# Constant operands of Vector's build work in PSUM, another order of the edge batches, one table zeroed before the other, and the last layer's units inside its sweeps

## The reference, cut to what matters

```
x = LN(x + three GCN layers(x, edge_weight) @ Wl + bl)
x = LN(x + two SAGE layers(x))
x = LN(x + sigmoid(decoder(relu(5 GRU steps(encoder(x))))))
x = LN(x + one GCN layer(x, unit weights) @ W + b)
# every layer sums h[src] over the edges into dst: segment_sum(h[src] * norm, dst)
```

## Time and profile before

| | us |
|---|---|
| median of 3 runs | 5748.14 (5744.3 to 5749.56) |
| the profiled execution | 5746.37 |
| its span, first to last instruction | 5744.6 |
| PE busy | 4803.0 (84%) |
| POOL busy | 2567.7 (45%) |
| DVE busy | 1751.7 (30%) |

### The profile page before, as it was taken

The page is one execution under the profiler, slowest core; times in us unless marked ns, Lnnn a source line. Parts: engine busy times, 40 slices in busy tenths (PEclk is TensorE's granted clock), DMA queues, the critical chain, the costliest instruction groups (busy, mean ns, idle before and its releaser), DMA issues. The chain is left out here.

```text
span 5744.6 us, 79088 instructions
## 1 busy us (share of the span) xinstructions
PE 4803.0 (84%) x25665; PEld 2581.3 (45%) x25665; DVE 1751.7 (30%) x3228; ACT 1204.8 (21%) x2507; POOL 2567.7 (45%) x1704
## 2 busy tenths in 40 slices
PE   3555555496299999999999998999999999997796
PEld 3555555242145444444454544444444444443343
DVE  9999999200000100010050303103030120303413
ACT  5555556100011111111120102112020110202200
POOL 4888888888888888888885000000000000000100
PEclk7555555697699999999999999999999999999897
DMA  9999983487399999999989785775858668582474
GB/s 352 358 354 353 351 238 52 119 240 220 49 303 302 270 300 289 301 273 299 288 235 298 242 294 185 224 254 182 299 174 271 215 222 268 172 299 74 146 261 135
DMA packets 717086, 1401.96 MB, mean 244 GB/s; under 512 B 268372, under 2 KB 356264, under 8 KB 691880
## 3 DMA queue, kind: packets, MB, share of 16 engines
q1 hardware_dynamic: 483832, 1346.10, 69.9%
q0 software_dynamic: 225216, 0.70, 7.6%
q10 hardware_dynamic: 7920, 53.79, 2.4%
HBM read 1160.09 MB, written 240.25 MB: 244 GB/s over the span
## 5 line engine op out<-in xcount | busy, mean ns | idle before, releaser
L837 PE MATMUL psum<-arena 128*128 128x512 f16 (+3 forms) x14014 | 3683.0, 424 | 299.4 <-issue 171.9
L837 PEld LDWEIGHTS psum<-arena 128*128 (+2 forms) x14014 | 1671.9, 124 | 2245.1 <-issue 1113.7
L548 POOL DMA_INDIRECT W_adj<-arena x782 | 1289.3, 1649 | 257.1 <-issue 239.1
L548 POOL DMA_INDIRECT C_adj<-arena x782 | 1213.9, 1552 | 240.1 <-issue 240.0
L680 POOL TENSOR_TENSOR arena<-arena 128x512 f32 (+1 forms) x13 | 22.1, 1700 | 1811.7 <-DVE arena L1172 1811.7
L427 DVE TENSOR_SCALAR_CACHE_REDUCE arena<-arena 128x2048 bf16<-128x2048 f32 (+7 forms) x392 | 709.5, 1875 | 0.6 <-issue 0.6
L497 PE MATMUL psum<-arena 128*128 (+1 forms) x6664 | 224.6, 167 | 482.7 <-DVE arena L449 459.4
L497 PEld LDWEIGHTS psum<-arena 128*128 128x128 bf16 x6664 | 213.7, 104 | 499.2 <-issue 450.3
L1356 DVE COPY arena<-psum 128x512 f32<-128x512 f32 (+1 forms) x39 | 23.2, 653 | 1353.5 <-PE psum L847 1159.4
L270 ACT ACTIVATE arena<-arena 128x1024 bf16<-128x1024 f32 (+7 forms) x392 | 298.5, 773 | 401.3 <-DVE arena L427 387.8
L1358 DVE TENSOR_SCALAR arena<-psum,arena 128x512 f32<-128x512 f32 x30 | 21.9, 748 | 1038.9 <-PE psum L837 1038.9
(11 more groups left out here) (233 smaller groups left out, 2594.5 us busy)
## 6 DMA issues: line engine op xcount, KB each, us to landing
arena<-C_adj SPq DMA_DIRECT2D x784, 384.0 KB
arena<-W_adj SPq DMA_DIRECT2D x294, 768.0 KB
arena<-C_adj SPq DMA_DIRECT2D x392, 512.0 KB
arena<-W_adj SPq DMA_DIRECT2D x147, 1024.0 KB
arena<-C_adj SPq DMA_DIRECT2D x392, 288.0 KB
arena<-W_adj SPq DMA_DIRECT2D x147, 576.0 KB
W_adj<-arena SPq DMA_DIRECT2D x12, 6400.0 KB
W_adj<-arena SPq DMA_DIRECT2D x12, 6144.0 KB
```

Source lines behind the costliest of these rows:

```text
L548: return pool.indirect_dma_start(table, bass.IndirectOffsetOnAxis(idx[:, t:t + 1], 0), values[:, t:t + 1], None, compute_op=ALU.add)
L837: ins = pe.matmul(psum[:, bank + b, 0:width], lhs, ring[:, slot, b * BANK:b * BANK + width], start=begin and part == 0, stop=False, skip_g ...
```

## The change: what it does, and the diff

Four edits. (1) `psRamp` and `psUpto` (f32, PSUM bank 2) and `psW` (f32, banks 4 and 5) are the constant operands of the five `compare` products in place of `rampb`, `upto` and `w`. The small block that works out `flight` and `ready` becomes `conflicts()` and is called after the first `merge` instead of before the first `compare`. (2) The batches come in the order 0, then groups 4g+2, 4g+4, 4g+1, 4g+3, and 45, 47, 46, 48 at the end. Here too no neighbours touch; the inputs then need 29, 37, 45 and 49 batches for the four sweeps (counted from the inputs). (3) SP writes zeros to all of W_adj, then to all of C_adj. (4) The stage `last` goes. In sweeps 1 to 3 of `decode` PE makes, after each of the first laps of eight chunks, the product of one unit of the sweep before; DVE and ACT normalise it, and ACT issues its output DMA. The three units of sweep 3 come after it. The products read `sum_fm` directly (no ACT copy), into PSUM banks 7 and 3, and the result lies where `h_fm` was.

```diff
+ORDER = [0] + [4 * g + u for g in range((NB - 5) // 4) for u in (2, 4, 1, 3)]
+ORDER += [b for u in (0, 1) for b in range(len(ORDER) + u, NB - 1, 2)] + [NB - 1]
...
+LAST_BANKS = (7, 3)
...
+    psRamp, psUpto = psum[:, 2, 0:P], psum[:, 2, P:2 * P]
+    psW = psum[:, 4:6, :].rearrange("p a b -> p (a b)")[:, 0:TILES]
...
-        for z in range(BLOCKS):
-            at_, width = z * BANK, block_width(z)
-            for table, of, zeroed in ((W_rows, zero, w_zeroed), (C_rows, z16, c_zeroed)):
+        for table, of, zeroed in ((W_rows, zero, w_zeroed), (C_rows, z16, c_zeroed)):
+            for z in range(BLOCKS):
+                at_, width = z * BANK, block_width(z)
                 for u, (c0, c1) in enumerate(halves):
...
-        dve.tensor_copy(rampb, ramp)
-        link(dve.tensor_scalar(upto, ramp, pcol[:, 0:1], None, ALU.is_ge))
+        dve.tensor_copy(psRamp, ramp)
+        dve.tensor_copy(psW, w)
+        link(dve.tensor_scalar(psUpto, ramp, pcol[:, 0:1], None, ALU.is_ge))
...
+        def conflicts():
             (the block of L402 to L418, indented)
...
-            dve.tensor_tensor(high, rampb[:, 0:CHUNKS].unsqueeze(1).to_broadcast([P, TB, CHUNKS]),
+            dve.tensor_tensor(high, psRamp[:, 0:CHUNKS].unsqueeze(1).to_broadcast([P, TB, CHUNKS]),
...
-            dve.tensor_tensor(ohl, rampb.unsqueeze(1).to_broadcast([P, TB, P]),
+            dve.tensor_tensor(ohl, psRamp.unsqueeze(1).to_broadcast([P, TB, P]),
...
-            dve.tensor_tensor(Et[:, slot, 0:half, :], near, upto.unsqueeze(1).to_broadcast([P, half, P]), ALU.mult)
+            dve.tensor_tensor(Et[:, slot, 0:half, :], near, psUpto.unsqueeze(1).to_broadcast([P, half, P]), ALU.mult)
...
-            dve.tensor_tensor(weighted, high, w[:, b * TB:(b + 1) * TB].unsqueeze(2).to_broadcast([P, TB, CHUNKS]),
+            dve.tensor_tensor(weighted, high, psW[:, b * TB:(b + 1) * TB].unsqueeze(2).to_broadcast([P, TB, CHUNKS]),
...
-            dve.tensor_tensor(Et[:, slot, half:, :], far, upto.unsqueeze(1).to_broadcast([P, half, P]),
+            dve.tensor_tensor(Et[:, slot, half:, :], far, psUpto.unsqueeze(1).to_broadcast([P, half, P]),
...
             merge(b, b % 2)
+            if b == 0:
+                conflicts()
...
-    return stages + [("gru", STEPS - 1, None), ("decode", None, (False, "ln", True)), ("last", None, None)]
+    return stages + [("gru", STEPS - 1, None), ("decode", None, (False, "ln", True))]
...
+            def last_product(j):                       # PE
+                if j >= 2:
+                    pe.wait_ge(s["products_read"], last.read + j - 1)
+                for c in range(chunks_of(j)):
+                    ins = pe.matmul(psum[:, LAST_BANKS[j % 2], c * D:(c + 1) * D],
+                                    sum_fm[:, (j * UC + c) * P:(j * UC + c + 1) * P], wt["L3W"], start=True, stop=True)
+                ins.then_inc(s["products"], 1)
...
-                    with pe.Fori(0, LAPS) as i:
+                    lap = 0
+                    if name == "decode":
+                        for j in blocks_of(sweep - 1):
+                            for u in range(LAP):
+                                chunk(lap * LAP + (u + 1), u, sweep, 16 * lap + 16 * (laps + 1))
+                            pe.wait_ge(s["sum_dve"], base.sum_dve)
+                            pe.wait_ge(s["sum_act"], base.sum_act)
+                            last_product(j)
+                            lap += 1
+                    with pe.Fori(lap, LAPS) as i:
...
+            if name == "decode":                       # after the last sweep
+                for j in blocks_of(SPLIT):
+                    last_product(j)
...
+            def last_unit(j):                          # ACT
+                root(j, last.norms)
+                act.wait_ge(s["unit_set"], last.units + j + 1)
+                act.dma_start(out[j * BANK:(j + 1) * BANK, :]..., nodes(result, j)).then_inc(s["out_written"], 16)
...
+            def last_unit(j):                          # DVE
+                dve.wait_ge(s["products"], last.products + j + 1)
+                ps = bank_nm(LAST_BANKS[j % 2])
+                for c in range(chunks_of(j)):
+                    ins = dve.scalar_tensor_tensor(out=work[:, c, :], in0=ps[:, c, :],
+                                                   scalar=dinv_c[:, j * UC + c:j * UC + c + 1],
+                                                   in1=x_nm[:, j * UC + c, :], op0=ALU.mult, op1=ALU.add)
+                ins.then_inc(s["products_read"], 1)
+                dve.wait_ge(s["products_read"], last.read + j + 1)
+                norm_at[0] = last.norms + j + 1
+                normalise(lambda c: result[:, j * UC + c, :], chunks_of(j))
+                dve.wait_ge(s["unit_set"], last.units + j + 1)
...
                     # ACT and DVE, in each sweep of decode, ahead of the copies of its sums
+                    if name == "decode" and sweep:
+                        for j in blocks_of(sweep - 1):
+                            last_unit(j)
...
-        return v[[b // 4 * 4 + (1, 3, 0, 2)[b % 4] if b < NB - 1 else b for b in range(NB)]].reshape(EDGES)
+        return v[ORDER].reshape(EDGES)
```

More of the change, by code:

```diff
@@ L159, in build_adjacency @@
     ends = take(P, [2, TILES], I32)
-    rest = take(P, [TILES], F32)
+    w, rest = take(P, [TILES], F32), take(P, [TILES], F32)
     cell, tmp = (take(P, [TILES], I32) for _ in range(2))
@@ L165, in build_adjacency @@
     far, near_ = take(P, [NB], F32), take(P, [NB], F32)
-    farthest, nearest, order = take(NB, [1], F32), take(NB, [1], F32), take(NB, [1], F32)
+    limits, order = take(NB, [SPLIT], F32), take(NB, [1], F32)
+    at[0] = end
+    farthest, nearest, needed, last_of = take(NB, [1], F32), take(NB, [1], F32), take(NB, [SPLIT], F32), take(SPLIT, [1], F32)
     reach, meets, meets2, landed_by = (take(1, [2, NB], F32) if i == 0 else take(1, [NB - 1], F32) for i in range(4))
-    limits, needed = take(NB, [SPLIT], F32), take(NB, [SPLIT], F32)
-    last_of = take(SPLIT, [1], F32)
-    at[0] = end
     key, flip = (take(P, [TILES], I32) for _ in range(2))
@@ L406, in vector @@
[L406 to L414, removed]
@@ L558, in stage_list, with last_layer, blocks_of, chunks_of @@
     stages += [("gru", n, (False, 1, False)) for n in range(STEPS - 1)]
-    return stages + [("gru", STEPS - 1, None), ("decode", None, (False, "ln", True)), ("last", None, None)]
+    return stages + [("gru", STEPS - 1, None), ("decode", None, (False, "ln", True))]
+def last_layer(stages):
+    last = Bases()
+    for stage in stages:
+        last.advance(*stage)
+    last.units = units_before(stages, len(stages))
+    return last
+def blocks_of(sweep):
+    first, n, _ = SWEEPS[sweep]
+    return range(first, first + n)
+def chunks_of(j):
+    return UC if j < UNITS - 1 else CHUNKS - UC * (UNITS - 1)
 class Bases:
@@ L574, in advance @@
         has = lambda *names: UNITS if name in names else 0
-        self.products += has("gcn", "sage", "enc", "gru", "decode", "last")
+        self.products += has("gcn", "sage", "enc", "gru", "decode")
         self.seconds += has("sage", "enc", "decode") + (UNITS if (name, arg) in
@@ L578, in advance @@
         self.features += UNITS if feeds else 0
-        self.inputs += has("gcn", "sage", "enc", "last")
+        self.inputs += has("gcn", "sage", "enc")
         self.gates += has("gru")
-        self.norms += UNITS if (name, arg) in (("gcn", 2), ("enc", 1)) or name in ("decode", "last") else 0
-        self.read += has("gcn", "sage", "enc", "gru", "last")
+        self.norms += UNITS if (name, arg) in (("gcn", 2), ("enc", 1)) or name == "decode" else 0
+        self.read += has("gcn", "sage", "enc", "gru")
 def run_layers(nc, io, sems, persist, take, at, psum, c_added):
@@ L647, in run_layers @@
     stages = stage_list()
+    last = last_layer(stages)
+    result = h_fm.rearrange("p (c f) -> p c f", f=D)
     def unit(ap, j):
@@ L756, in products @@
             def products(j, q):
-                if name in ("gcn", "last", "sage", "enc"):
+                if name in ("gcn", "sage", "enc"):
                     wait_read(j, 2)
@@ L770, in products @@
                         else:
-                            rhs = wt["L3W"] if name == "last" else (wt["W1"], wt["W2"], W3l)[arg]
+                            rhs = (wt["W1"], wt["W2"], W3l)[arg]
                         ins = pe.matmul(psum[:, 4 + q, sl], sum_in[:, q, sl], rhs, start=True, stop=True)
@@ L979, in scalar @@
             wide = feeds is not None and feeds[0]
-            norm = (name, arg) in (("gcn", 2), ("enc", 1)) or name in ("decode", "last")
+            norm = (name, arg) in (("gcn", 2), ("enc", 1)) or name == "decode"
             base_units = units_before(stages, k)
@@ L985, in lead @@
             def lead(j, q):
-                if name in ("gcn", "sage", "enc", "last"):
+                if name in ("gcn", "sage", "enc"):
                     if not isinstance(j, int) or j >= 2:
@@ L1158, in vector, with normalise @@
```

(22 more changed lines are left out.)

63 lines of the change are left out of this document (33 added, 30 removed).

## The result

The changed kernel takes **5604.19 us** (median of 6 runs, 5599.94 to 5607.22) against 5747.17 for the kernel before (6 runs on the same chip): a ratio of 0.9751, 95% interval [0.9739, 0.9764]. Its profiled execution took 5599.94 us, with a span of 5598.2. The forecast was 5575, so 143 us came and not 172. The order of the steps is as forecast; 29 us are missing.

The account below looks back on a forecast made before the run. It took PE as the bound from about 1719 us, with POOL's adds gating three sweeps before. 5746.4 - 119.0 (sweeps) - 54.3 (last layer) = 5573.1, and 1.8 for the median: 5575; 8 in 10 range 5550 to 5622.

Parts of the forecast that it names:

- POOL's relief: PSUM operands stop DVE's build products delaying POOL's adds: 3.33 us a batch, 92.4 us at every start from batch 29 on.
- DVE's price: In the build, the two bf16 products slow to 1217 ns each with an f32 PSUM operand: 52.4 us over 49 batches.
- Order: First stage: first three sweeps need two batches less each; third sweep starts at 1434.8, fourth at 1566.9 instead of 1719.0.
- C's gate: First C stage's last sweep waits for POOL's last add, starts at 3021.7; 31.4 of the 152.1 us are given back.
- Zeros: The new order of zeroing W_adj and C_adj was counted as worth 0 us.
- Tail: After the last sweep's matmuls, 16.0 us remain instead of 80.8: 64.8 us gained.
- the products in the sweeps: Last layer: ten products of 1.05 us moved into the sweeps add 10.5 us to PE's path.
- units disturb the sweeps: Rival: PE waits in each lap for the unit's DVE work, ten units cost 55 us, not 10.5; 5619, chance 0.05.
- slower by PSUM: Rival: PSUM operands read at two cycles an element, 289 us more in the build, which then gates; 5807, chance 0.03.
- POOL not relieved: Rival: PSUM constants leave POOL's delays in the build, only order and tail help; 80.9 us gained, 5667, chance 0.07.
- The price limit: Extra DVE build time has 55 us of cover: it decides from 1.1 us a batch above forecast, slower kernel from 4.7.

## Why the prediction was right, and what was 29 us off

*POOL's relief, 92.4 us.* The mechanism is shown: putting only the ramp back into SBUF returned 46 of the 78 us of delay. The size was too large; this is the term that was off. I took 3.33 us a batch as the difference between the build's rate and the idle rate, and then moved the whole later chain rigidly. But the build's stretch of the earlier trace rows holds three gaps behind every 112th add, 4.4, 4.5 and 3.4 us long, and the idle stretch only two of 1.3 and 1.2. The difference counted them as relief, and PSUM operands do not remove them: they are 4.3, 2.9 and 6.2 afterwards. Batch 35 starts at 1139.0 where the forecast gives 1130.1: 8.9 us. The gaps inside the changed build, 4.0, 2.6 and 5.9 longer than a usual step, are 12.5 in all, where the rate of DVE's idle time, 29.86 a batch against 29.72 between gaps, has 26 x 0.14 = 3.6. Up to batch 35 the adds take 945.4 us before and 867.2 after, POOL's small products 35.0 and 25.9, and its idle time is 190.0 and 193.3: 84.0 less in all. Then the 561st add met the load burst, which starts as DVE's build ends: 17 us. In the kernel before the 561st add came at 1222, some 70 us after the burst's end. Relief and the place of the burst are not independent, and I treated them so.

*DVE's price, 52.4.* Right to 0.01 us a product (1210 for 1217 ns), and sweep 0 to 1.4 us (1106.5 for 1105.1). The Trainium skill's page "VectorE: DVE Perf Modes", section "The perf-mode tier table", gives a `tensor_tensor` with an operand in PSUM half the rate of bf16 in SBUF; 1210 against 682 ns agrees. What I missed is that the price bought nothing for these two products, and that its real effect on the time was indirect: through the burst's place.

*Of POOL's reading of the earlier trace rows* ("two SBUF tensors stop an add, a PSUM operand doesn't"): shown, with 47 undisturbed starts in the long product against 38 and 34 delayed ones. The rows it was read from were weaker than they looked: the trace has 33 adds that begin inside L1206 and L1220, not 22, but these last 0.34 us, and an end 1.42 us behind theirs would have delayed an add by 0.2 at most. The Trainium skill's page "SBUF — State Buffer", section "Who interferes with whom", has an instruction of DVE with at most one SBUF input not contend, and one with two contend with GpSimd instructions that read SBUF; the delays of the adds agree. DVE itself was hardly slowed: L442 takes 2.28 us with either operand, and only where an add started within 0.04 us of a product of two SBUF tensors did the product grow, by 0.05 to 0.07 us.

*Order.* Two gates gone and one left, as said; the third sweep at 1460.9 for 1434.8 (26.1 late, all of it POOL's), the fourth at 1592.1 for 1566.9 (25.2).

*C's gate.* There, as forecast; it is no accident of size. From batch 45 of W to the last add of C are 1592 us of POOL, from the third sweep to the last C sweep 1554 us of PE. So in the new order, whenever the first gate decides, the second takes back some 35 us: 37.2 here and 37.1, 35.4, 36.3, 33.3 and 36.3 in the five experiments where it did. I had 31.4; POOL's C part has 5 us more in gaps than before. Hence 3052.0 for 3021.7, 30.3 late.

*Zeros* 0: right. *Tail* 15.4 for 16.0, *the products in the sweeps* 9.1 for 10.5: PE runs 190.1 us from 5392.7 to the sweeps' end, where it ran 181.0 before. Right; together they are 2.0 better than forecast.

*Sum.* 30.3 late at C's gate, less 2 from the tail's terms, are 28.3; the profiled execution is 26.8 above the 5573.1 of the sum. The remaining 1.5 I leave unexplained. The median lies 4.2 above the profiled execution, the fastest of the six, where the forecast added 1.8: hence 29 and not 27. Of the rivals, "units disturb the sweeps" and "slower by PSUM" have no trace, "POOL not relieved" is refuted by its adds. The price limit was mis-sized too: DVE's work had 91.7 us of cover and not the 55 of the prediction, in part because POOL came late. That the time stayed inside the range is partly luck: the range did not name what filled it, a term whose timing depends on another.

What stays open: what sets the small gaps behind every 112th add inside the build, beyond the packets still to come (6 us at most in the changed kernel, 8 in others of nearly the same POOL work), why POOL stops at every 112th add at all, and what sets the gap's size inside a burst, beyond the packets still to come: 841 of them make 14.5 us, 1100 make 20.0, and 1206 only 15.8.

## What to carry to other kernels

Give an operand to PSUM only for those DVE instructions that the helped engine really collides with, and count hits in the trace instruction by instruction: here the 2.28 us product cost POOL 67 of 78 us, and the two 0.68 us ones 11 (1.6 in the kernel that has only them back in SBUF). When you speed up one producer, don't shift the later chain rigidly: look which periodic wait of it now falls into a burst of another queue. Before paying for or saving on a covered engine, find the second gate of the same producer; with two gates on one chain the time is that chain's end, and earlier work before the first gate only lengthens the waits.

## What the runs showed of the hardware

- An indirect add that starts inside a DVE product of two SBUF tensors ends 1.41 to 1.44 us after the product (all 38 inside the 2.28 us product of the kernel before and all 34 with the ramp back in SBUF); beside a product with one PSUM operand it lasts 1.55 as ever (47 starts in L442, 45 in L449 and L454). An add that starts within 0.04 us of the start of a product of two SBUF tensors is not delayed; the product takes 1.02 to 1.04 us for 0.97 (11 in the kernel with the ramp back in SBUF).
- Indirect adds beside 8 KB loads get one packet for one of the loads: 51.6 packets a microsecond instead of the 79.6 that POOL issues. The loss costs POOL time only if a 112th add comes before the backlog is gone, then as 14 to 20 us of idle time put down to "issue" (five kernels); in the seven others up to 1506 packets waited without a stop.
- A bf16 product of 1024 elements takes 0.68 us from SBUF and 1.21 with an f32 operand in PSUM; an f32 product of 2048 takes 2.28 with either.
